# Softmax shifts placed per half unit from ScalarE's queue, with the second scores six slots behind the first

## What is computed

```
x = x + tanh(g0) * attention0(layernorm(x), ctx)      # 16 heads, softmax
x = x + tanh(g1) * experts0(layernorm(x))             # 8 experts + 1 shared, top 4
x = x + tanh(g2) * attention1(layernorm(x), ctx)      # the same, scores clipped to +-10000
x = x + tanh(g3) * experts1(layernorm(x))             # 8 experts, top 2, hidden 1024
attention:  s = clip((q k^T) / 4);  p = softmax(s);  out = (p v) Wo + bo
```

## Time and profile before

| what | value |
|---|---|
| median of 3 runs | 982.74 us (978.57 to 985.58) |
| the profiled execution | 982.38 us |
| its span in the trace | 980.6 us |
| mean granted clock of PE over the span | 0.951 of full speed |
| PE, DVE, ACT, POOL busy | 905.1, 740.2, 471.6, 252.5 us |

### The profile page before, as it was taken

The page is one execution under the profiler, slowest core; times in us unless marked ns, Lnnn a source line. Parts: engine busy times, 40 slices in busy tenths (PEclk is TensorE's granted clock), DMA queues, the critical chain, the costliest instruction groups (busy, mean ns, idle before and its releaser), DMA issues.

```text
span 980.6 us, 18579 instructions
## 1 busy us (share of the span) xinstructions
PE 905.1 (92%) x6641; PEld 746.2 (76%) x6641; DVE 740.2 (75%) x1516; ACT 471.6 (48%) x835; POOL 252.5 (26%) x385
## 2 busy tenths in 40 slices
PE   7998999999999998999988877899899999999995
PEld 6766677777767766777756554667799999999995
DVE  4555767677676767798887898978868788887783
ACT  2245544444534343344433444443356666666773
POOL 7511011020210000010101113323136566543331
PEclk9999999999999999999999977769799999999998
DMA  6977866146152346474655873342387777777772
GB/s 167 181 147 153 185 184 118 48 80 110 41 78 56 63 83 106 76 154 98 130 115 101 186 210 106 96 125 63 121 266 221 215 217 220 221 220 217 231 249 44
DMA packets 128523, 139.69 MB, mean 142 GB/s; under 512 B 12336, under 2 KB 121160, under 8 KB 128304
## 3 DMA queue, kind: packets, MB, share of 16 engines
q1 hardware_dynamic: 119296, 127.59, 52.5%
q0 software_dynamic: 7488, 10.39, 5.0%
q10 hardware_dynamic: 1648, 0.53, 0.3%
HBM read 108.50 MB, written 29.44 MB: 141 GB/s over the span
## 4 chain that ended last, share of the span: by engine, by line
PE 65%; DVE 18%; issue 5%; DMA 4%; ACT 3%; POOL 2%; SPq 1%; POOLq 0%; DVEq 0%; ACTq 0%
PE bank L1024 11%; PE bank L849 9%; PE by_query L1008 7%; PE by_key L1008 7%; PE bank L859 5%; DVE rowmax L1368 4%; PE value_bank L791 4%; PE by_query L752 3%; DVE probs L1393 3%; PE bank L694 3%; PE bank L738 2%; PE bank L818 2%; PE by_key L773 2%; PE bank L703 2%; DMA lower<-lower 2%
## 5 line engine op out<-in xcount | busy, mean ns | idle before, releaser
L1162 ACT ACTIVATE probs<-by_key 128x1024 f32<-128x1024 f32 x128 | 130.7, 1021 | 99.3 <-PE by_key L773 98.8
L1368 DVE TENSOR_REDUCE rowmax<-by_query 128x4 f32<-128x1024 f32 x128 | 155.6, 1215 | 27.5 <-PE by_query L752 27.5
L1903 POOL TENSOR_SCALAR rstd<-moments 128x2 f32<-128x2 f32 x32 | 10.5, 327 | 490.3 <-DVE moments L1324 490.2
L1970 POOL DMA_INDIRECT out_x<-x,token_i x39 | 68.7, 1763 | 124.3 <-ACT x L1271 94.2
L752 PE MATMUL by_query<-stack_k,stack_q 48*128 48x256 f32 x512 | 67.3, 342 | 25.3 <-DVE rowmax L1368 23.7
L1024 PE MATMUL bank<-w_hi,h_hi 128*128 128x256 f32 x312 | 88.3, 283 | 0.0
L1024 PE MATMUL bank<-w_lo,h_hi 128*128 128x256 f32 x312 | 88.3, 283 | 0.0
L1024 PE MATMUL bank<-w_hi,h_lo 128*128 128x256 f32 x312 | 88.3, 283 | 0.0
L752 PEld LDWEIGHTS by_query<-stack_k,stack_q 48*128 48x128 f32 x512 | 40.3, 194 | 63.0 <-DVE rowmax L1368 35.3
L791 PE MATMUL value_bank<-probs,values 128*32 128x256 f32 x1024 | 76.9, 423 | 10.5 <-DVE probs L1393 10.3
L859 PE MATMUL bank<-w_down,hidden 128*128 128x256 f32 x288 | 79.8, 400 | 3.8 <-DVE summed L1431 1.8
(11 more groups left out here) (267 smaller groups left out, 2257.8 us busy)
## 6 DMA issues: line engine op xcount, KB each, us to landing
w<-in_L_ffn_W SPq DMA_DIRECT2D x46, 1024.0 KB, 7.3
lower<-lower SPq DMA_DIRECT2D x64, 256.0 KB, 5.5
stack_k<-qk SPq DMA_DIRECT2D x96, 128.0 KB, 4.9
stack_q<-qk SPq DMA_DIRECT2D x96, 128.0 KB, 6.7
qk<-hi SPq DMA_DIRECT2D x31, 256.0 KB, 2.4
qk<-lo SPq DMA_DIRECT2D x31, 256.0 KB, 2.7
rows<-w_gate SPq DMA_DIRECT2D x8, 264.0 KB, 4.7
x<-in_x SPq DMA_DIRECT2D x8, 256.0 KB, 6.4
```

Of the source, the lines that this page charges most:

```text
L1162: ac.activation(probs[i % 4][:, :, :, :].rearrange("p k h s -> p h k s"), by_key[:, :, :].rearrange("p h (k s) -> p h k s", k=2), ACT.Exp) ...
L1368: dv.tensor_reduce(rowmax[u % 2][:, :, p, :], by_query[:, :, :].rearrange("p h (t s) -> p h t s", t=TT), AX, ALU.max).then_inc(sem.max_don ...
L1970: po.indirect_dma_start(out[:, :], bass.IndirectOffsetOnAxis(ap=token_i[:, n:n + 1].bitcast(U32), axis=0), ysb[i % 3][:, t, :], None, comp ...
```

## The change

LAG goes from 10 to 6. The shifts are made, turned and placed for half a unit (four pairs, HP) at a time: n = 2u + half counts 32 groups. The group's turn stands at half slot g + 8 + 8 half, that is in slots base(u) + 4 and base(u) + 8. The high and the low part of a side lie in neighbouring rows, so two transfers of 16 rows of 512 bytes, each to two rows of stack_q, place a group, and ScalarE issues them itself after its copy; in layer 1 it also stores the group's bounds. SP places nothing any more. Second scores wait for their own half. The query work of the last unit and the last stages stand eight half slots earlier, and the rotation of the banks starts at another bank.

```diff
-LAG = 10
+LAG = 6
+HP = PAIRS // 2
+HROWS = H * TT // 2
...
-            at[g - 23].append(("stats", ("query", u)))
-            at[g - 21].append(("normal", ("query", u)))
-            at[g - 19].append(("turn", ("query", u)))
-            at[g - 16 if u > 1 else g - 15].append(("qprod", u))
+            early = 8 if u == UNITS - 1 else 0
+            at[g - 23 - early].append(("stats", ("query", u)))
+            at[g - 21 - early].append(("normal", ("query", u)))
+            at[g - 19 - early].append(("turn", ("query", u)))
+            at[g - 16 - early if u > 1 else g - 15].append(("qprod", u))
...
-        at[g + 16].insert(0, ("shift_turn", u))
+        for half in range(2):
+            at[g + 8 + 8 * half].insert(0, ("shift_turn", 2 * u + half))
...
-    at[g - 20].append(("load_alternative", 0))
-    at[g - 13].append(("any_nan", 0))
-    at[g - 11].append(("spread_nan", 0))
+    at[g - 28].append(("load_alternative", 0))
+    at[g - 21].append(("any_nan", 0))
+    at[g - 19].append(("spread_nan", 0))
     for b in range(NB):
-        g = 2 * base(UNITS - 1) - 9 + FINISH_STEP * b
+        g = 2 * base(UNITS - 1) - 17 + FINISH_STEP * b
...
-            bank_of[stage, n] = (i % 3, bank_release(*uses[i - 3]) if i >= 3 else None)
+            bank_of[stage, n] = ((i + 2) % 3, bank_release(*uses[i - 3]) if i >= 3 else None)
...
-    lower_dram = nc.dram_tensor("lower", (NB, H * TT, P), F32).ap()
+    lower_dram = nc.dram_tensor("lower", (NB, 2, HROWS, P), F32).ap()
...
-    rowmax = [sba(f"rowmax{i}", [P, 2, PAIRS, TT]) for i in range(2)]
-    shift = sba("shift", [P, 3, H * TT])
-    shiftT = sba("shiftT", [3 * H * TT, P])
+    rowmax = [sba(f"rowmax{i}", [P, 2, HP, TT]) for i in range(4)]
+    shift = sba("shift", [P, 3, HROWS])
+    shiftT = sba("shiftT", [3 * HROWS, P])
...
-        def place_shift(u):
-            l, b = layer_of(u), batch_of(u)
-            sp.wait_ge(sem.shiftT_ready, u + 1)
-            for side in range(2):
-                for part in range(2):
-                    row, src = HALF * side + FULL + part, (2 * part + side) * PAIRS * TT
-                    sp.dma_start(stack_q[u % SETS][row:row + 1, :, :].bitcast(F32).rearrange("o a (t q) -> o (a t) q", t=TT),
-                                 shiftT[src:src + PAIRS * TT, :]).then_inc(sem.shift_in, 16)
-            if l:
-                sp.dma_start(lower_dram[b], shiftT[2 * H * TT:3 * H * TT, :]).then_inc(sem.lower_out, 16)
-
...
-            sp.wait_ge(sem.lower_out, 16 * (b + 1))
+            half, pair = divmod(p, HP)
+            sp.wait_ge(sem.lower_out, 16 * (2 * b + half + 1))
...
-            if p == 0:
-                pe.wait_ge(sem.shift_in, 64 * (u + 1))
+            if p % HP == 0:
+                pe.wait_ge(sem.shift_in, 32 * (2 * u + p // HP + 1))
...
+        def shift_turn(n):
+            if n:
+                ac.wait_ge(sem.shift_in, 32 * n)
+            if n > 2 * NB:
+                ac.wait_ge(sem.lower_out, 16 * (n - 2 * NB))
+            bank, bounds = banks[BANK_OF["shift_turn", n][0]], slice(2 * HROWS, 3 * HROWS)
+            ac.wait_ge(sem.shift_turned, n + 1)
+            if n >= 2 * NB:
+                ac.activation(shiftT[bounds, :], bank[bounds, 0:P], ACT.Exp)
+            ac.activation(shiftT[0:2 * HROWS, :], bank[0:2 * HROWS, 0:P], ACT.Copy).then_inc(sem.shiftT_ready, 1)
+            u, half = divmod(n, 2)
+            ac.wait_ge(sem.shiftT_ready, n + 1)
+            for side in range(2):
+                row, src = HALF * side + FULL, side * HROWS
+                ac.dma_start(stack_q[u % SETS][row:row + 2, HP * half:HP * half + HP, :].bitcast(F32).rearrange(
+                    "o a (t q) -> o (a t) q", t=TT), shiftT[src:src + HROWS, :]).then_inc(
+                    sem.shift_in, 16)
             if layer_of(u):
-                ac.activation(shiftT[bounds, :], bank[bounds, 0:P], ACT.Exp)
-            ac.activation(shiftT[0:2 * H * TT, :], bank[0:2 * H * TT, 0:P], ACT.Copy).then_inc(sem.shiftT_ready, 1)
+                ac.dma_start(lower_dram[batch_of(u), half], shiftT[2 * HROWS:3 * HROWS, :]).then_inc(sem.lower_out, 16)
...
-                if q == PAIRS - 1:
-                    shifts(v)
+                if q % HP == HP - 1:
+                    shifts((PAIRS * v + q) // HP)
```

More of the change, by code:

```diff
@@ L575, in load_lower @@
                 sp.wait_ge(sem.clip_done, j - 2)
-            sp.wait_ge(sem.lower_out, 16 * (b + 1))
-            sp.dma_start(lower[j % 3][:, :, :], lower_dram[b].rearrange("(h a t) q -> a h (t q)", h=2, t=TT)[p]
+            half, pair = divmod(p, HP)
+            sp.wait_ge(sem.lower_out, 16 * (2 * b + half + 1))
+            sp.dma_start(lower[j % 3][:, :, :], lower_dram[b, half].rearrange("(h a t) q -> a h (t q)", h=2, t=TT)[pair]
                          .partition_broadcast(P)).then_inc(lower_in[j % 3], 16)
@@ L634, in _ @@
         stages = {"load": load, "ctx": context, "kprod": store_keys, "qprod": store_queries, "stack_keys": stack_keys, "stack_queries": stack_queries,
-                  "shift_turn": place_shift, "mean_project": store_alternative, "project": store_z, "reload": reload, "load_expert": load_expert, "load_alternative": load_alternative,
+                  "mean_project": store_alternative, "project": store_z, "reload": reload, "load_expert": load_expert, "load_alternative": load_alternative,
                   "weights1": store_rows, "bias1": store_x, "tables": first_weights}
@@ L754, in scores_by_query @@
             mm.then_inc(sem.qk1_done, 1)
[L756 to L759, removed]
+        def shift_turn(n):
+            bank = open_bank("shift_turn", n)
+            pe.wait_ge(sem.shift_ready, 2 * (n + 1))
+            pe.transpose(bank[0:3 * HROWS, 0:P], shift[:, :, :].rearrange("p j r -> p (j r)"),
                          ident[:, :]).then_inc(sem.shift_turned, 1)
@@ L1364, in maxima @@
             i = PAIRS * u + p
-            if p == 0 and u >= 2:
-                dv.wait_ge(sem.shift_ready, 2 * (u - 1))
+            half, pair = divmod(p, HP)
+            if pair == 0 and u >= 2:
+                dv.wait_ge(sem.shift_ready, 2 * (2 * (u - 2) + half + 1))
             dv.wait_ge(sem.qk1_done, i + 1)
-            dv.tensor_reduce(rowmax[u % 2][:, :, p, :], by_query[:, :, :].rearrange("p h (t s) -> p h t s", t=TT),
+            dv.tensor_reduce(rowmax[(2 * u + half) % 4][:, :, pair, :], by_query[:, :, :].rearrange("p h (t s) -> p h t s", t=TT),
@@ L1369, in maxima, with shifts @@
                              AX, ALU.max).then_inc(sem.max_done, 1)
-        def shifts(u):
-            flat = rowmax[u % 2][:, :, :, :].rearrange("p h a t -> p (h a t)")
-            dv.wait_ge(sem.max_done, PAIRS * (u + 1))
-            if layer_of(u):
-                dv.tensor_scalar(flat, flat, CLAMP, -CLAMP, ALU.min, ALU.max).then_inc(sem.shift_chain, 1)
-                dv.wait_ge(sem.shift_chain, u + 1 + batch_of(u))
-            if u:
-                dv.wait_ge(sem.shift_turned, u)
-            dv.tensor_scalar(shift[:, 0, :].bitcast(F32R), flat, -1.0, None, ALU.mult).then_inc(sem.shift_chain, 1)
-            dv.tensor_scalar(shift[:, 2, :], flat, -1.0, -CLAMP, ALU.mult, ALU.add).then_inc(sem.shift_ready, 1)
-            dv.wait_ge(sem.shift_chain, u + 1 + (batch_of(u) + 1 if layer_of(u) else 0))
-            dv.scalar_tensor_tensor(shift[:, 1, :].bitcast(F32R), flat, -1.0, shift[:, 0, :], ALU.mult,
+        def shifts(n):
+            flat = rowmax[n % 4][:, :, :, :].rearrange("p h a t -> p h (a t)")
+            by_side = shift[:, 0:2, :].rearrange("p j (o r) -> p (j o) r", o=2)
+            hi, lo = by_side[:, 0:4:2, :], by_side[:, 1:4:2, :]
+            done = n + max(n - 2 * NB, 0)
+            dv.wait_ge(sem.max_done, HP * (n + 1))
+            if n >= 2 * NB:
+                dv.tensor_scalar(flat, flat, CLAMP, -CLAMP, ALU.min, ALU.max).then_inc(sem.shift_chain, 1)
+                done += 1
+                dv.wait_ge(sem.shift_chain, done)
+            if n:
+                dv.wait_ge(sem.shift_turned, n)
+            dv.tensor_scalar(hi.bitcast(F32R), flat, -1.0, None, ALU.mult).then_inc(sem.shift_chain, 1)
+            dv.tensor_scalar(shift[:, 2, :].rearrange("p (h r) -> p h r", h=2), flat, -1.0, -CLAMP, ALU.mult, ALU.add).then_inc(sem.shift_ready, 1)
+            dv.wait_ge(sem.shift_chain, done + 1)
+            dv.scalar_tensor_tensor(lo.bitcast(F32R), flat, -1.0, hi, ALU.mult,
```

## The result

The changed kernel takes 1016.09 us (median, 1010.61 to 1023.03), the kernel before 982.4 us on the same chip: ratio 1.0348, 95% interval 1.0272 to 1.0425. The forecast of 978.1 us (965 to 993) was wrong.

What follows compares the result with a forecast made beforehand. PE was taken as the bound beside the first layer's experts, DVE after them. Terms -12.5 + 4.2 - 3 + 2.5 + 2.5 + 2 = -4.3 took 982.4 to 978.1 us, range 965 to 993.

Steps and rivals of the forecast that it cites:

- Step 1: Start of attention: experts begin four slots earlier, 14.6 us of ramp less 2.1 us net to pay, -12.5 us.
- step 7: Placement of shifts: the way takes 3.8 us, the tightest two slots 4.65, so no cost, 0 us.
- Rival B: Start held by DMA stack loads: only 6.4 of 12.5 us come, 984 us in total; chance 0.12.
- Step 2: After the experts: four full slots more and four tail slots less, +4.2 us.
- step 3: Units interleave differently: half of two clip waits for the load of the bounds goes, -3 us.
- Steps 4 and 5: 16 more turns on PE, +2.5 us; more groups of small operations on DVE, +2.5 us.
- the 752 named: Sign for DVE: a busy time over 752 us would upset the cost of its small operations.
- Step 6: ScalarE issues the placement: 46 us more work there, nearly all hidden in its waits, +2 us.
- Rival C: ScalarE's queue delays tanh or split, then DVE, banks and PE: +23 in place of +2, 999 us; chance 0.13.
- Rival D: Two-row transfers of the shifts land late, at most 5 us more, 983 us in total; chance 0.05.

Runs made afterwards that it cites:

- e4: Changed kernel with LAG 8 in place of 6 and SP issuing all transfers of the halves: 980.9 us, ratio 0.9981 to the kernel before.
- e9: e4 with three filler products behind the maxima in slots 8 and 9: 980.2 us, ratio 0.9987 to the kernel before.
- e5: Changed kernel with LAG back at 10 and SP issuing all transfers of the halves: 983.3 us, ratio 1.0025 to the kernel before.
- e10: Kernel before without the filler of slots 8 and 9, nothing else changed: 987.2 us, ratio 1.0054 to the kernel before.
- e12: Changed kernel, still at LAG 6, with every transfer issued by SP and none by ScalarE: 1012.4 us, ratio 1.035 to the kernel before.
- e8: Changed kernel with ScalarE doing the query's split before the second half's shift copy and issues: 1004.3 us, ratio 1.0228 to the kernel before.
- e1: Changed kernel with LAG back at 10, ScalarE still issuing the halves: 1006.4 us, ratio 1.026 to the kernel before.
- e7: e2 with SP holding the next unit's stack loads until the first half is placed: 1046.7 us, ratio 1.0716 to the kernel before.
- e6: e2 with each first half in four one-row transfers, not two of two rows: 1017.9 us, ratio 1.0422 to the kernel before.
- e2: Changed kernel with the second half's transfers issued by SP, the first half's by ScalarE: 998.9 us, ratio 1.0172 to the kernel before.

## Why the prediction was wrong, step by step

*Step 1 (four slots less at the start, -12.5): failed.* The stretch became 5.8 us longer; even with PE waiting 0.9 us or not at all for transfers it is 2.8 (e4) and 0.3 us (e9) longer than before with two slots less, and 1.5 longer in e5 with none less. I charged 2.1 us net for four slots' second scores, by PE's busy time. Three things in that were wrong. The shift rows land late, which I had at nothing: PE waits 10.6 us for them there (step 7). What is added stands ahead of the products on which splits and maxima hang, so that two slots alone cost 2.0 and 1.0 us more (e9). And the filler, which I booked as 4.2 us saved, held the clock up: leaving out half of that much alone cost 5.3 us (e10). Rival B saw a start that gives less than 12.5 us, but had it 6.4 us shorter, and its reason was not the one: PE waited 0.2 us for the stack loads.

*Step 2 (+4.2) and step 3 (-3): not settled.* Together they say +1.2 us; the stretch behind the experts grew by 5.0. With SP issuing it reads 126.5, 121.0 and 125.5 us at six, eight and ten slots (e12, e4, e5), with no trend, and e10, which changed nothing there, is 1.8 over the kernel before. The waits for the bounds' load (5.9 us, three times) are gone in the changed kernel, all of them, where I took half. In their place the weighing of values waits 11.3 us for clipped exponentials behind the experts, before 6.8. The tail behind the last maxima is 19.4 us, forecast 22.

*Steps 4 and 5 (+5 together): borne out.* e5, which has the turns, the small DVE operations and the two-row transfers, costs 2.5 us over the kernel before; its interval (0.9994 to 1.0056) holds the 5 us and holds no change. DVE is busy 747.0 us, under the 752 named.

*Step 6 (ScalarE issues, +2): mis-sized, and the largest error.* It measured 23 us at ten slots and 11 at eight (there mostly through the exponentials behind the split); at six slots the ratios of the changed kernel and e12 are alike, as SP pays with L what ScalarE pays with Q. One issue takes 0.62 us, not the 0.49 of the earlier trace rows. The failure is in the cover: I held 106 and 99 us of ScalarE's waits against 46 us of work. But those waits stand before tanh and exponential, while the issues stand behind an exponential and before the split. There, in the kernel before, the copy ends at 443.3 us and the split begins at 443.7, which leaves 0.4 us to spare for 1.7 us of issues:

```profile
443.05 0.27 ACT L1151 ACTIVATE shiftT<-bank 64x128 f32<-64x128 f32 x1
...
443.69 0.48 ACT L1074 ACTIVATE hi<-bank,qkb 128x256 fp32r<-128x256 f32 x1 [0.37 <-PE bank L738]
```

Over all units ScalarE waits 12.9 us in 14 times before this split, 0.9 each and the longest 3.0. e8 shows that the place matters, not the sum. Rival C named this chain (split late, DVE's half late, bank not free, PE stands) and its price, +21 over the forecast, close to e1's 23; I gave it 0.13. The Trainium skill ("DMA: Bandwidth & Descriptors", Issuing engines are not separate DMA queues) says that issuing from several engines saves only the sequencer's time. The runs agree in kind: what moves is 0.62 us an issue, and who pays for it is decided by the order on the engine that takes it over.

*Step 7 (placement in time, 0): failed.* I compared 3.8 us of way with 4.65 us of slots and took the landing of 2.2 us from transfers issued five slots behind the stack loads. One slot behind them it is 5.9 to 6.9 us in the chain (1.9 when they are held, e7). The step that I left out was to ask what is in flight at the new place. Rival D named the symptom (waits at p = 0) at 5 us, where the changed kernel has 11.5; its reason, that each transfer writes two rows, is refuted by e6, whose one-row transfers land no sooner.

The parts don't add up. At six slots SP's order makes L worse as it removes Q (e12), and a split of the two (e2) is the best at that lag.

**What stays open.** Between e4 and e12, both with SP alone issuing, the stretch beside the experts grows from 434.6 to 444.1 us. It is not waiting: PE's waits in it sum to 21.5 and 21.9 us, only 0.9 of these for the shift rows. PE is busy longer, 411.9 and then 421.2 us:

```profile
111.40:546.00 434.60, 411.89 (x2779) 309.58 (x2777) 338.91 (x815) 189.92 (x365) 43.63 (x141) 0.99 0.48 101
```
```profile
120.90:565.00 444.10, 421.24 (x2788) 317.66 (x2790) 339.73 (x815) 189.94 (x363) 44.64 (x141) 0.98 0.47 99
```

Of the 9.3 us, 3.5 are in the products with wkv, of which eight more fall into the stretch, as it begins two slots earlier, and 5.0 in gate_up's, which are as many as before and take longer. The granted clock is 0.80 in e12's first 10.1 us, just after PE waited for shift rows, and 1.00 in e4's first 10.0. No run has six slots with the shift rows on time and all else in place, and none shows why ScalarE's issues cost more at ten slots than at eight.

No version beats the kernel before. e4 and e9 are level with it, with intervals that hold 1.

## What to carry to other kernels

A transfer's landing time belongs to the place where it is issued, so before moving one, list what is in flight there, on every queue. Hold an engine's added work against the wait directly behind it in its order, not against the sum of its waits. And a shorter distance between two stages gives nothing where the work it pulls forward stands ahead of what the next step waits for, still less if filler that held the clock up goes with it.

## What the runs showed of the hardware

A transfer of 16 rows of 512 bytes within the core, issued on ScalarE's queue 0.1 us after 12 loads of 128 KB were issued on SP's, took 6.6 us in the chain and not the 1.9 of e7, where the loads were held: another queue gave no way past the loads, and four one-row transfers fared no better than two two-row ones (5.0 to 7.6 us in e6's chain, 4.6 to 7.9 in e2's). After 14 of the 108 filler products on by_key were left out (e10), PE's granted clock was at its lower level from 62 to 66 us. The busy time of the whole stretch hides this, 21.0 of 23.0 us against 21.1 before, since products take longer at the lower clock; the 4 us ahead of the fall show it, 1.6 us busy against 3.1.
